# Who multiplies the fourth head's probabilities by their reciprocal sum: VectorE or ScalarE

## The reference

```python
# attention: 32 query heads in 8 groups of 4, 512 cached keys and 128 new ones
q, k, v = x @ Wq.T, x @ Wk.T, x @ Wv.T       # 32, 8 and 8 heads of 128
q, k = rope(rmsnorm(q)), rope(rmsnorm(k))
k_all, v_all = concat(paged_cache, new)      # 640 keys
scores = q @ k_all.T / sqrt(128); scores[cached and past the length] = -1e30
probs = softmax(scores)                      # exp(...) times 1 / its row sum
x1 = x + ffn((probs @ v_all) @ Wo.T)         # ffn: silu gate, upper half by size set to 0, up, down
out = x1 + int4_linear(adapter_linear(x1))
```

## Time and profile before

| | |
|---|---|
| median of 3 runs | 1373.96 us (1373.55 to 1375.35) |
| the profiled execution | 1373.65 us |
| its span, first to last instruction | 1371.8 us |
| granted TensorE clock | 1.00 |
| chain of work that ended last | PE 91%, DVE 5%, ACT 2% |

### The profile page before, as it was taken

The page is one execution under the profiler, slowest core; times in us unless marked ns, Lnnn a source line. Parts: engine busy times, 40 slices in busy tenths (PEclk is TensorE's granted clock), DMA queues, the critical chain, the costliest instruction groups (busy, mean ns, idle before and its releaser), DMA issues.

```text
span 1371.8 us, 23449 instructions
## 1 busy us (share of the span) xinstructions
PE 1356.9 (99%) x8015; PEld 1183.4 (86%) x8015; DVE 1203.7 (88%) x2624; ACT 871.3 (64%) x2224; POOL 784.2 (57%) x813
## 2 busy tenths in 40 slices
PE   9899999999999999999999999999999999999998
PEld 6788888888888888888888888888888888888888
DVE  8999898989898989898989898989899987987783
ACT  7777676767676767676767676767777662222221
POOL 7876666666667666766676667666766510111111
PEclk9999999999999999999999999999999999999999
DMA  6111211121112111111111111112121321111212
GB/s 220 45 51 43 58 55 47 43 58 53 49 41 59 54 48 43 58 55 47 43 59 55 47 43 59 54 48 74 45 71 32 110 96 45 47 47 49 76 42 75
DMA packets 34050, 80.46 MB, mean 59 GB/s; under 512 B 10274, under 2 KB 11554, under 8 KB 32514
## 3 DMA queue, kind: packets, MB, share of 16 engines
q1 hardware_dynamic: 17538, 45.29, 10.3%
q0 software_dynamic: 16384, 33.59, 8.0%
HBM read 76.74 MB, written 2.10 MB: 57 GB/s over the span
## 4 chain that ended last, share of the span: by engine, by line
PE 91%; DVE 5%; ACT 2%; issue 1%; POOL 0%; DVEq 0%; ACTq 0%
PE proj_ps L111 10%; PE proj_ps L113 10%; PE proj_ps L112 10%; PE turn_ps L772 10%; PE score_ps L113 5%; PE score_ps L112 5%; PE score_ps L111 5%; PE value_ps L111 5%; PE value_ps L112 5%; PE value_ps L113 5%; PE gu_ps L111 3%; PE gu_ps L113 3%; PE gu_ps L112 3%; PE out_ps L1037 2%; PE turn_ps L734 2%; PE turn_ps L741 2%
## 5 line engine op out<-in xcount | busy, mean ns | idle before, releaser
L1288 ACT ACTIVATE probs<-probs,shift,rstd 128x640 f32<-128x640 f32 x256 | 234.4, 918 | 120.2 <-DVE shift L1732 119.1
L563 POOL DMA_INDIRECT kg<-kc,idx x256 | 259.8, 1015 | 83.8 <-issue 77.9
L573 POOL DMA_INDIRECT vg<-vc,idx x256 | 260.3, 1017 | 70.7 <-issue 70.6
L1768 DVE TENSOR_TENSOR pt_lo<-turn_ps,pt_hi 128x512 fp32r<-128x512 f32 x320 | 217.4, 685 | 45.4 <-ACT pt_hi L1294 44.9
L1294 ACT ACTIVATE pt_hi<-turn_ps 128x512 fp32r<-128x512 f32 x320 | 187.6, 593 | 93.6 <-PE turn_ps L772 93.0
L1743 DVE CUSTOM_DVE_ANT_0 probs<-score_ps,mask 128x640 f32<-128x640 f32 x256 | 206.8, 822 | 12.0 <-PE score_ps L113 10.2
L581 POOL TENSOR_TENSOR v_lo<-vg,v_hi 128x512 fp32r<-128x512 f32 x64 | 89.1, 1391 | 207.5 <-ACT v_hi L1259 207.4
L772 PE MATMUL turn_ps<-cst,probs 128*128 128x128 f32 x1280 | 191.5, 272 | 1.7 <-DVE probs L1761 1.0
L111 PE MATMUL proj_ps<-w_hi,xt_parts 128*128 128x512 f32 x496 | 189.1, 381 | 0.7 <-ACT qk L1244 0.7
L772 PEld LDWEIGHTS turn_ps<-cst,probs 128*128 128x128 f32 x1280 | 157.1, 140 | 28.2 <-DVE probs L1761 2.2
L113 PE MATMUL proj_ps<-w_hi,xt_parts 128*128 128x512 f32 x496 | 168.2, 339 | 0.0
(11 more groups left out here) (255 smaller groups left out, 3283.4 us busy)
## 6 DMA issues: line engine op xcount, KB each, us to landing
w_raw<-wqkv SPq DMA_DIRECT2D x28, 384.0 KB, 3.2
wo_raw<-wo SPq DMA_DIRECT2D x32, 256.0 KB, 3.1
wa_sb<-wa SPq DMA_DIRECT2D x7, 1024.0 KB, 4.8
kg<-kc,idx POOLq DMA_INDIRECT x256, 2.6
vg<-vc,idx POOLq DMA_INDIRECT x256
wg_raw<-wg SPq DMA_DIRECT2D x2, 1376.0 KB, 6.1
wu_raw<-wu SPq DMA_DIRECT2D x1, 2752.0 KB, 9.3
wd_raw<-wd SPq DMA_DIRECT2D x1, 2560.0 KB, 12.6
```

The lines of the kernel that those rows point to most:

```text
L563: pool.indirect_dma_start(kg[:, b % 2, c, :], None, kc, bass.IndirectOffsetOnAxis(ap=idx[:, s // B % 2, b * NC + c:b * NC + c + 1], axis=0))\
L573: pool.indirect_dma_start(vg[:, b % 2, c, :], None, vc, bass.IndirectOffsetOnAxis(ap=idx[:, s // B % 2, b * NC + c:b * NC + c + 1], axis=0))\
L1288: act.activation(row, row, ACT.Exp, bias=shift[:, h:h + 1], scale=rstd[:, b % 2, h:h + 1], accum_out=sums[:, h:h + 1])\
L1768: dve.tensor_tensor(pt_lo[:, at, :], turn_ps[1 - j % 2][:, :], pt_hi[:, at, :].bitcast(F32), ALU.subtract).then_inc(p_lo_done[j], 1)
```

## The change

For tiles 3 to 63 ACT does the product of the fourth head (number 3): an ACTIVATE Copy with the reciprocal as scale. It stands in ACT's order after the exponentials of heads 2 and 3 and ahead of the rounding of block 3, and it waits for the reciprocal. DVE's `normalise` leaves that head out; its `probs_done` comes with head 2's product. A new semaphore `last_head_done` goes to PE (block 0) and to DVE (ahead of the next reciprocal, which overwrites `recips`). The key numbers now count on `table_in`, so that all who wait for it wait for three DMAs.

```diff
+BY_ACT = 3
-                    sp.dma_start(key_no, consts[:, C_KEY:C_ALL]).then_inc(key_in, 16)
+                    sp.dma_start(key_no, consts[:, C_KEY:C_ALL]).then_inc(table_in, 16)
@@ PE, turn_probs
                         if j == 0:
                             wait(pe, probs_done, s + 1)
+                            wait(pe, last_head_done, s + 1 - BY_ACT)
@@ ACT
+                    def normalise_last(s, b):
+
+                        if s >= BY_ACT:
+                            wait(act, recip_done, s + 1)
+                            row = probs[:, b % 2, REP - 1, :]
+                            act.activation(row, row, ACT.Copy, scale=recips[:, REP - 1:REP]).then_inc(last_head_done, 1)
@@ ACT, step
                         if live(s + 1):
                             exps(s + 1, b1, (2, 3))
+                        if live(s + 1):
+                            normalise_last(s + 1, b1)
@@ ACT and DVE, three places: hide_keys, signed_weights, tables
-                        act.wait_ge(key_in, 16)
+                        act.wait_ge(table_in, 3 * 16)
@@ DVE, normalise
                             wait(dve, exp_done[REP - 1], s + 1)
+                            wait(dve, last_head_done, s - BY_ACT)
                             dve.reciprocal(recips[:, :], sums[:, :]).then_inc(recip_done, 1)
                             wait(dve, recip_done, s + 1)
+                        by_act = s >= BY_ACT
                         for h in heads:
-                            row = probs[:, b % 2, h, :]
-                            last = dve.tensor_scalar(row, row, recips[:, h:h + 1], None, ALU.mult)
-                        if h == REP - 1:
-                            last.then_inc(probs_done, 1)
+                            if h < REP - by_act:
+                                row = probs[:, b % 2, h, :]
+                                last = dve.tensor_scalar(row, row, recips[:, h:h + 1], None, ALU.mult)
+                                if h == REP - 1 - by_act:
+                                    last.then_inc(probs_done, 1)
```

More of the change, by code:

```diff
@@ L135, in adaln_attn_ffn @@
         table_in = semaphore("table_in")
-        key_in = semaphore("key_in")
         x_in = [semaphore(f"x_in{n}") for n in range(4)]
@@ L185, in adaln_attn_ffn @@
         probs_done = semaphore("probs_done")
+        last_head_done = semaphore("last_head_done")
         p_turned = [semaphore(f"p_turned{j}") for j in range(NJ)]
@@ L1399, in signed_weights @@
                         lo, hi = slice(0, D // 2), slice(D // 2, D)
-                        act.wait_ge(table_in, 2 * 16)
+                        act.wait_ge(table_in, 3 * 16)
                         for n, factor in enumerate((1.0, float(D) ** 0.5)):
@@ L1789, in tables @@
                         bs = TABLE_GROUPS[0]
-                        dve.wait_ge(table_in, 2 * 16)
+                        dve.wait_ge(table_in, 3 * 16)
                         ta, tb, factor = ((qa, qb, 1.0), (ka, kb, float(D) ** 0.5))[n]
```

## The result

The changed kernel takes 1379.21 us (median of 6 runs, 1378.24 to 1381.89) beside 1374.41 for the kernel before (6 runs, 1373.55 to 1375.35): ratio 1.0038, 95% interval 1.0028 to 1.0047. Predicted were 1379.1. From median to median it is 4.8 us more; the prediction had added 5.4 to the one profiled execution of 1373.65. In the sets of the experiments 1 to 8 and 12 the kernel before itself took 1489 to 1519 us, so there a ratio is taken within its set, and step lengths are read only in the steps that kept theirs (5, 13, ... 53, 61 and 62).

The account below looks back on a forecast made before the run. PE, busy 1356.9 of 1371.8 us, bounds the kernel; the new product delays pt_lo, which PE awaits. Terms 0.3 + 1.2 + 1.5 + 0.4 - 0.3 + 0 + 0.5 + 0.9 + 0.9 = 5.4, on 1373.65: 1379.1; range 1375.5 to 1384.

Parts of the forecast that it names:

- The price of the ACTIVATE: ACT's new 128x640 Copy with a scale operand: 0.82 us, bounds 0.73 and 0.92.
- rival 1: ACT's product costs as much as the exponential, 0.92 us: 9.3 us lost, 1383; chance 0.17.
- rival 2: ACT's idle 0.81 us hides the product (0.73 or a little over): 3.2 or 2.3 us lost, 1376; chance 0.15.
- The ladder and its deadline: Reciprocal, product, block 3's rounding, pt_lo ending at +2.26; no PE loss if L734 is due at +2.37 or later.
- tight steps: Steps 3, 6, 14, ... 54 lose 0.15 each, 1.2 us; steps 8, 16, ... 56 lose 0.22 each, 1.5 us.
- slack of 0.04 in ordinary steps: L734 is due 2.41 after the reciprocal, against 2.37 needed: loss 0, with 0.04 us to spare.
- The semaphore at nothing: Key numbers share a semaphore with two norm weights; DVE's tables wait for a third DMA: 0 to 0.34, taken as 0.
- Relief in steps 12, 20, ... 52: PE's wait for kt_lo, 0.38 a step, stays despite lighter DVE, because w_lo waits for ACT's w_hi: gain 0.
- Rival 3: DVE's relief wins: kt_lo follows DVE's own queue in steps 12 to 52 and 55 to 60; 3.9 us, 1369.8; chance 0.08.
- estimate of 0.3 for block 4's pt_lo: Ordinary steps: block 4's pt_lo comes up to 0.15 later; 0.3 us lost in all, from 0 to 1.
- Steps 55 and 57 to 60: Gate weights are split, kt_lo already late: about 0.1 more in each, 0.5 us lost.
- Step 2: First step with the product; L734 is due 1.96 after the reciprocal: a loss of 0.4 us.

Follow-up runs that it names:

- experiments 1 to 8 and 12: Follow-up kernels edited from the kernel before or the changed kernel, in sets where the kernel before itself took 1489 to 1519 us.
- experiment 2: Kernel before with VectorE's product of the fourth head left out for tiles 3 to 63, on any engine; 2118 us, ratio 1.42.
- experiment 7: Changed kernel with one more one-column ScalarE instruction ahead of each product except the last tile's; 1506.00 beside 1490.80, ratio 1.0100.
- experiment 11: Changed kernel with three one-column ScalarE instructions ahead of every product, the last tile's too; 1393.81 beside 1374.85, ratio 1.0139.
- Experiment 10: Changed kernel with ScalarE's product issued behind its rounding of block 3 instead of ahead of it; 1375.32 beside 1374.85, ratio 1.0002.
- Experiment 1: Kernel before with key numbers, qw and kw counted on one shared semaphore, no product moved; 1488.30 beside 1489.35, ratio 0.9991.
- first profile: Profile of the changed kernel, nothing further edited, from the first set of runs; this profiled execution took 1380.01 us.
- second profile: Profile of the changed kernel, nothing edited, from a second set taken later; that set gave 1378.80 beside 1374.85, ratio 1.0031.
- 9 to 11: Changed kernel unedited, 1378.80; with its product behind block 3's rounding, 1375.32; with three one-column instructions ahead of every product, 1393.81; kernel before 1374.85 us.

## Why the prediction was right

**The bound.** That DVE's share was no bound was right: the product left out gave nothing in the steps that can be read (experiment 2), and with 31.9 us less on DVE no ordinary step became shorter.

**The price of the ACTIVATE.** 0.83 us by the trace, 0.82 from like rows; rival 1 (0.92) and rival 2 (0.73) fall by the first row of it. The group's mean is 831 ns. The estimate by the Trainium skill ("ScalarE: Activation LUTs", What ACT_TABLE_LOAD costs), 0.81, is off by 0.02.

**The ladder and its deadline.** Its end and the 0.11 us that PE needs held to about a hundredth: turns at +2.29 or +2.30 in the tight steps and in step 61, each with the later start of 0.06 inside the group, and at +2.59 in an ordinary step with 0.30 added. The slack of 0.04 in ordinary steps, the riskiest figure since 31 ordinary steps hang on it (the prediction counted 28), is measured: 0.10 more cost 0.04 to 0.07 (experiment 7), 0.30 more cost 0.22 to 0.25 in nearly all (experiment 11), so 0.03 to 0.08 are free. Experiment 10 shows the cause: take the rung out and leave all else, and the time is back.

**The semaphore at nothing.** Experiment 1 does not speak against it but is too coarse for a few tenths. The starts say more, and they do not follow the semaphore: block 1 of step 0 is turned at 36.33 and 35.85 in the two profiles of the change, at 35.91 before, and DVE's tables began at 13.65 in the first profile and at 13.17 in the second, at 13.23 before.

**Relief in steps 12, 20, ... 52.** Rival 3 fell where it was to decide. In step 36 of the changed kernel, first ACT, then DVE, then PE, to be read with the earlier trace rows:

```profile
668.94 1.05 ACT L1234 ACTIVATE w_hi<-w_raw 128x1024 fp32r<-128x1024 f32 x1
...
670.02 1.23 DVE L1669 TENSOR_TENSOR w_lo<-w_raw,w_hi 128x1024 fp32r<-128x1024 f32 x1 [0.25 <-ACT w_hi L1234]
...
668.95 0.66 PE L735 MATMUL turn_ps<-cst,kg 128*128 128x128 f32 x4
...
671.91 0.33 PE L748 MATMUL turn_ps<-cst,rot_k 128*128 128x128 f32 x1
```

w_lo starts 0.03 behind w_hi's end, as before; DVE has 0.25 us of idleness ahead of it where it had none marked before, and this is where a part of the relief went. From turn to turn it is 2.96, as against 2.95.

**What was off.** The sum was 0.7 us high, from small terms. The estimate of 0.3 for block 4's pt_lo should have been 0: of 0.15 that it could come later nothing reached PE. Steps 55 and 57 to 60 lost 0.18, not 0.5: only step 58 paid (0.15); in 55, 57 and 59 every matmul of PE stands within 0.03 of its old place in the step, in 60 within 0.05. I had charged them by analogy, without following DVE's queue in one of them. Step 2 lost 0.19 and not 0.4, though its turn of the cached keys did come 0.40 later in the step (0.34 and 0.06 inside the group). The loss was given back behind it, where PE already waited before. The end of the score matmuls and the start of the output projection in step 2, first of the kernel before, then of the second profile:

```profile
87.19 0.31 PE L113 MATMUL score_ps<-kt_hi,qt_lo 128*128 128x320 f32 x1
87.48 0.47 PE L111 MATMUL proj_ps<-wo_hi,ot_hi 128*128 128x512 f32 x1
87.79 0.40 PE L112 MATMUL proj_ps<-wo_lo,ot_hi 128*128 128x512 f32 x1
```

```profile
87.51 0.31 PE L114 MATMUL score_ps<-kt_hi,qt_lo 128*128 128x320 f32 x1
87.66 0.39 PE L112 MATMUL proj_ps<-wo_hi,ot_hi 128*128 128x512 f32 x1
87.89 0.39 PE L113 MATMUL proj_ps<-wo_lo,ot_hi 128*128 128x512 f32 x1
```

Before, the projection starts 0.29 and 0.31 behind its neighbours, after 0.15 and 0.23: 0.22 of a hidden wait is used up. The step had 17.52 for an ordinary 17.13, and I should have asked where those 0.39 stood before charging all of the new loss. Step 62 lost 1.04 for 0.9. That the median came out so close is luck: 5.4 was 0.7 too much by the profiles, and it was added to a profiled execution that lay 0.8 under the median of six. Besides, three of the six runs held a granted clock of 1.0 and took 1378.24 to 1378.78, which is near 1373.65 + 4.7 = 1378.35; the other three, at 0.998 or 0.999, took 1379.64 to 1381.89.

## What to carry to other kernels

Before work is moved to an idler engine, write down for the exact place in its queue what stands behind it and when that is due; here 0.8 us of idle time stood ahead of a rounding, and filling it cost 4.7 us, while the place one instruction further on cost 0.6, too little to be told from nothing by the total. An engine at 88% may still have nothing to give: a step is shortened only if PE's last wait ends there, and the rows must show that wait. A short kernel-wide loss can sit in a few steps, so compare step lengths by their position in the loop, not their mean.

## What the hardware showed unexpectedly

**A lower clock behind a wait.** Both profiles of the changed kernel have the same wait of 2.2 us in step 1, ahead of any product on ScalarE. First profile, PE:

```profile
62.52 0.50 PE L112 MATMUL value_ps<-pt_hi,v_hi 128*128 128x512 f32 x1 [2.23 <-DVE pt_lo L1782]
62.86 0.57 PE L113 MATMUL value_ps<-pt_lo,v_hi 128*128 128x512 f32 x1
63.22 0.63 PE L114 MATMUL value_ps<-pt_hi,v_lo 128*128 128x512 f32 x1
```

Second profile, PE:

```profile
62.01 0.50 PE L112 MATMUL value_ps<-pt_hi,v_hi 128*128 128x512 f32 x1 [2.20 <-DVE pt_lo L1782]
62.34 0.39 PE L113 MATMUL value_ps<-pt_lo,v_hi 128*128 128x512 f32 x1
62.57 0.39 PE L114 MATMUL value_ps<-pt_hi,v_lo 128*128 128x512 f32 x1
```

PE in a stretch behind that wait, first profile and second (us, busy time and count, granted clock, DMA share, GB/s):

```profile
62.90:66.30 3.40, 3.40 (x13) 0.50 0.13 42
```

```profile
61.40:64.80 3.40, 2.79 (x16) 1.00 0.18 49
```

In the first, the granted clock fell to its lower level (1.2 GHz) for these 3.4 us and step 1 took 21.68 us; in the second it did not and step 1 took 19.86 (19.88 before). The same code at the same place, 1.8 us apart. Step 2 behind it is 0.4 shorter in the first (17.29 for 17.71), so 1.4 of the 1.7 between the two spans, 1378.2 and 1376.5, come from here. Such a dip is not the change's: experiment 1, where no product moves, has it in step 1 too (21.86 us, granted clock 0.50 from 62.7 to 66.1). A comparison of two single profiles would have put it down to the change.

**A condition that the clock does not show.** Where before took 1489 us, ACT waited in most steps for something that the profile names only as remote. ACT in step 7 of experiment 1 (the code of before but for one semaphore):

```profile
181.32 0.60 ACT L1293 ACTIVATE pt_hi<-turn_ps 128x512 fp32r<-128x512 f32 x1 [0.80 <-PE turn_ps L771]
184.03 0.60 ACT L1293 ACTIVATE pt_hi<-turn_ps 128x512 fp32r<-128x512 f32 x1 [2.12 <-remote]
185.45 0.60 ACT L1243 ACTIVATE qk<-proj_ps 128x512 f32<-128x512 f32 x1 [0.82 <-remote]
186.88 0.60 ACT L1270 ACTIVATE kt_hi<-turn_ps 128x512 fp32r<-128x512 f32 x1 [0.83 <-remote]
```

The last three start 1.42 and 1.43 us apart, with idle time ahead of each; the step takes 19.86 us and not 17.13, while the granted clock is 0.994 over the run. By the program the row at 184.03 waits for PE's turn of block 4, and PE had been done with it at 181.81 + 0.60 = 182.41, 1.6 us earlier:

```profile
181.81 0.60 PE L771 MATMUL turn_ps<-cst,probs 128*128 128x128 f32 x4
```

Such waits of ACT stand in 47 of the 63 steps from turn to turn, in none of the kernel before at 1374 us, and never in steps 5, 13, ... 53, 61 and 62. The record gives another chip for each set of experiments: 1 to 4, 5 to 8 and 12 ran on three chips, all with the kernel before at 1489 us or more, and 9 to 11 on a fourth, with 1375 us. Whether the chip or the hour makes the difference can't be told from that. The cause is open.
